# Reordering the last three tiles of an FP4 FFN: one down product moved behind the last gate and up products, the last tile quantised and transposed in two column ranges

## The reference

```python
def fp4_quant_dequant(x):          # blocks of 16 along the last dim
    scale = jnp.maximum(jnp.max(jnp.abs(xb), axis=-1, keepdims=True) / 6.0, 1e-12)
    idx = jnp.searchsorted(_MID, jnp.abs(xb / scale))
    return (_GRID[idx] * jnp.sign(xn) * scale).reshape(shape)
def fp4_linear(x, w):
    return jnp.einsum('bsk,nk->bsn', fp4_quant_dequant(x), fp4_quant_dequant(w))
h = jax.nn.silu(fp4_linear(x, w_gate)) * fp4_linear(x, w_up)     # 512 -> 1408
out = x1 + gb * fp4_linear(h, w_down)                            # 1408 -> 512
```

## Time and profile before

| | us |
|---|---|
| three runs | 2029.9, 2030.3, 2032.15 |
| median | 2030.3 |
| the profiled execution | 2029.9 |
| its span in the trace | 2027.6 |
| TensorE busy in the span | 1947.3 (96%) |
| VectorE busy | 1705.7 (84%) |
| GpSimd busy | 1211.9 (60%) |
| ScalarE busy | 626.6 (31%) |
| mean granted TensorE clock (1 = 2.4 GHz) | 0.983 |

### The profile page before, as it was taken

How to read it: one execution, slowest core, us unless ns; L and a number is a source line. 1 busy time by engine, 2 the same in 40 slices (tenths; PEclk the granted TensorE clock), 3 DMA queues, 4 the chain that set the end, 5 groups by cost and what they waited for, 6 DMA issues and landing times.

```text
span 2027.6 us, 27098 instructions
## 1 busy us (share of the span) xinstructions
PE 1947.3 (96%) x9401; PEld 930.6 (46%) x9401; DVE 1705.7 (84%) x2080; ACT 626.6 (31%) x878; POOL 1211.9 (60%) x1083
## 2 busy tenths in 40 slices
PE   4889999999999999999999999999999999999996
PEld 2334444444444444444444444444444444444442
DVE  4767676868767999999999999999999999999974
ACT  2234343433322323233233233332332333323321
POOL 2245454646444667677677676676776766767721
PEclk7999999999999999999999999999999999999998
DMA  7945646464643343333433433434334334333242
GB/s 252 292 112 160 183 130 172 141 174 130 180 111 99 68 103 70 83 91 70 91 84 70 104 70 81 95 71 89 87 70 102 73 77 98 70 86 88 65 85 49
DMA packets 417867, 219.26 MB, mean 108 GB/s; under 512 B 356214, under 2 KB 356226, under 8 KB 417804
## 3 DMA queue, kind: packets, MB, share of 16 engines
q1 hardware_dynamic: 417804, 218.44, 43.1%
HBM read 96.48 MB, written 33.57 MB: 64 GB/s over the span
## 4 chain that ended last, share of the span: by engine, by line
PE 81%; DVE 6%; SPq 4%; DMA 3%; issue 3%; POOL 2%; ACT 1%; POOLq 0%; DVEq 0%; ACTq 0%
PE bank L892 44%; PE bank L913 22%; PE bank L839 14%; SPq L355 2%; SPq L419 2%; DMA arena<-arena 1%; PE bank L864 1%; DVE arena L963 1%; DVE arena L1072 1%; DMA arena<-in_L_attn_W_qkva_dram 1%; DMA arena<-in_L_ffn_w_down_dram 1%; DMA arena<-in_L_ffn_w_up_dram 1%; POOL arena L508 1%; POOL arena L506 0%; DVE arena L1099 0%
## 5 line engine op out<-in xcount | busy, mean ns | idle before, releaser
L892 PE MATMUL bank<-wgu_hi,arena 128*128 128x512 f16 (+1 forms) x3072 | 870.0, 362 | 0.0
L892 PE MATMUL bank<-wgu_lo,arena 128*128 128x512 f16 (+1 forms) x1536 | 555.5, 362 | 0.0
L839 PE MATMUL bank<-arena,wq_hi 128*128 128x512 f16 x1536 | 463.5, 384 | 15.2 <-DMA arena<-arena 8.4
L913 PE MATMUL bank<-wd_hi,arena 128*128 128x512 f16 x1408 | 432.4, 381 | 18.1 <-DMA arena<-arena 18.1
L892 PEld LDWEIGHTS bank<-wgu_hi,arena 128*128 128x128 f16 x3072 | 300.8, 98 | 308.1 <-issue 0.5
L839 PE MATMUL bank<-arena,wq_lo 128*128 128x512 f16 x768 | 294.2, 383 | 0.0
L913 PE MATMUL bank<-wd_lo,arena 128*128 128x512 f16 x704 | 268.5, 381 | 0.0
L839 PEld LDWEIGHTS bank<-arena,wq_hi 128*128 128x128 f16 x1536 | 151.0, 99 | 196.5 <-issue 17.5
L603 POOL TENSOR_TENSOR arena<-arena 128x512 f32<-128x512 f32 x64 | 154.1, 2408 | 123.9 <-DVE arena L1241 123.9
L913 PEld LDWEIGHTS bank<-wd_hi,arena 128*128 128x128 f16 x1408 | 138.5, 98 | 187.3 <-DMA arena<-arena 14.0
L892 PEld LDWEIGHTS bank<-wgu_lo,arena 128*128 128x128 f16 x1536 | 150.4, 98 | 153.9 <-issue 0.2
(11 more groups left out here) (129 smaller groups left out, 2602.9 us busy)
## 6 DMA issues: line engine op xcount, KB each, us to landing
arena<-in_L_attn_x_dram SPq DMA_DIRECT2D x32, 1024.0 KB, 6.4
arena<-x_scratch SPq DMA_DIRECT2D x128, 256.0 KB, 3.2
x_scratch<-arena SPq DMA_DIRECT2D x16, 1024.0 KB, 4.4
out_dram<-arena SPq DMA_DIRECT2D x64, 256.0 KB, 3.0
arena<-in_L_wmod_dram SPq DMA_DIRECT2D x6, 1024.0 KB, 8.8
arena<-in_L_attn_W_qkva_dram SPq DMA_DIRECT2D x1, 3072.0 KB, 15.1
wgu_hi<-in_L_ffn_w_gate_dram SPq DMA_DIRECT2D x1, 2816.0 KB, 13.5
wgu_lo<-in_L_ffn_w_up_dram SPq DMA_DIRECT2D x1, 2816.0 KB, 10.4
```

The lines of the kernel that those rows point to most:

```text
L839: last = pe.matmul(dst[m % 2][:, :].rearrange("p (j t) -> p j t", j=NJ), w[:, k, at], uT[p][:, half, :, k, :], start=(n == 0), stop=(n == ...
L892: last = pe.matmul(dst[n][:, 0:w], xT[p][:, half, k, :], wt[:, k, cut], start=(m == 0), stop=(m == 3 * KD - 1))
L913: last = pe.matmul(d_bank[p][:, :], hT[p][:, half, k, :], wt[:, k, :], start=(m == 0), stop=(m == 3 * KF - 1))
```

## The change

Only the last three tiles (61, 62 and 63, `LAST = 63`) are touched. The loops over all other tiles issue what they issued.

- TensorE: tile 63 no longer has `down(61)` between its first and second chunk. After the tile come `down(61)`, `down(62)` and `down_last()`. `down_last` has the 33 matmuls of `down(63)`, with the 22 on the high half first and the 11 on the low half behind them; each part waits for its own two transposes.
- VectorE: in tile 62 `gate_out(61)` is left out. Tile 63 is `last_tile()`: the quantisation runs over the column ranges `H_PARTS` = 0 to 1024 and 1024 to 1408. The first range goes as far as `h_y` before the third chunk's `hidden`; `gate_out(61)` comes between `h_quantised` and `h_lo`. After the tile follow `gate_out(62)`, `gate_out(63)` and the residual addition of tile 63.
- ScalarE: in tile 63 `steps_of_h` and `h_hi` are issued for each range; the third chunk's `silu` stands behind the first range's `steps_of_h`.
- GpSimd: `ffn_add_x(61)` moves behind tile 63, and `ffn_add_x(63)` is gone (VectorE does it).
- SP: `turn_h(63)` becomes four transposes (8 and 3 blocks of the high half, 8 and 3 of the low half), each with its own wait. `store(61)`, `load_residual(63)` and `store(62)` are issued behind them.

```diff
+                def turn_last():
+                    wait(sp, down_ready, LAST - 1)
+                    sp.nop(nofuse=True)
+                    for half, done, loaded in ((0, h_hi_ready, last_hi_loaded), (1, h_lo_ready, last_lo_loaded)):
+                        for n, (c0, c1) in enumerate(H_PARTS):
+                            sp.wait_ge(done, LAST + 1 + n)
+                            sp.nop(nofuse=True)
+                            sp.dma_start(hT[1][:, half, c0 // P:c1 // P, :], h_half[1][:, half, c0:c1],
+                                         transpose=True).then_inc(loaded, 16)
...
-                for t in range(NTA - 7, NTA):
+                for t in range(NTA - 7, LAST - 1):
                     slot(t, t % 2)
-                store(NTA - 1, 1)
+                turn_h(LAST - 1, 0)
+                turn_last()
+                store(LAST - 2, 1)
+                load_residual(LAST, 1)
+                store(LAST - 1, 0)
+                sp.wait_ge(last_x2_ready, 1)
+                sp.dma_start(out_tile[LAST], gated[1]).then_inc(out_stored[1], 16)
...
                 def tile(i, p, b, first, last, b3, b4):
+                    if b == B - 1 and last:
+                        for n, (c0, c1) in enumerate(H_PARTS):
+                            silu(i, p, b, n + 1)
+                            steps_of_h(i, p, n, slice(c0, c1))
+                        for n, (c0, c1) in enumerate(H_PARTS):
+                            h_hi(i, p, n, slice(c0, c1))
+                        return
...
+                def down_last():
+                    pe.wait_ge(last_hi_loaded, 16 * len(H_PARTS))
+                    pe.wait_ge(gated_ready, LAST - 1)
+                    for k in range(KF):
+                        for wt in (wd_hi, wd_lo):
+                            pe.matmul(d_bank[1][:, :], hT[1][:, 0, k, :], wt[:, k, :],
+                                      start=(k == 0 and wt is wd_hi), stop=False)
+                    pe.wait_ge(last_lo_loaded, 16 * len(H_PARTS))
+                    for k in range(KF):
+                        last = pe.matmul(d_bank[1][:, :], hT[1][:, 1, k, :], wd_hi[:, k, :],
+                                         start=False, stop=(k == KF - 1))
...
-                    if not (isinstance(i, int) and i < 2):
+                    if not (isinstance(i, int) and (i < 2 or i == LAST)):
                         down(i - 2, p)
...
-                down(NTA - 2, 0)
-                down(NTA - 1, 1)
+                down(LAST - 2, 1)
+                down(LAST - 1, 0)
+                down_last()
...
+                def last_tile():
+                    at = [(n, slice(c0, c1)) for n, (c0, c1) in enumerate(H_PARTS)]
+                    for n, cut in at:
+                        hidden(LAST, 1, B - 1, n + 1)
+                        h_max(LAST, 1, n, cut)
+                        h_scale(LAST, 1, n, cut)
+                        h_recip(LAST, 1, n, cut)
+                        if cut.stop == F:
+                            h_largest(LAST, 1, n)
+                            h_power(LAST, 1)
+                        h_y(LAST, 1, n, cut)
+                    for n, cut in at:
+                        h_magic(LAST, 1, n, cut)
+                        h_round(LAST, 1, n, cut)
+                    for n, cut in at:
+                        h_quantised(LAST, 1, n, cut)
+                    gate_out(LAST - 2, 1, B - 1)
+                    for n, cut in at:
+                        h_lo(LAST, 1, n, cut)
...
                 tiles(dve, tile)
-                gate_out(NTA - 1, 1, B - 1)
+                gate_out(LAST - 1, 0, B - 1)
+                gate_out(LAST, 1, B - 1)
+                dve.wait_ge(x_res_loaded[1], 8 * (LAST - 1) + 16)
+                dve.wait_ge(gated_ready, LAST + 1)
+                dve.tensor_tensor(gated[1], gated[1], x_res[1], ALU.add).then_inc(last_x2_ready, 1)
```

More of the change, by code:

```diff
@@ L303, in adaln_block_kernel @@
         NTA = B * NT
+        LAST = NTA - 1
+        H_PARTS = ((0, 2 * GT), (2 * GT, F))
         g_bank, up_bank, d_bank = [bank[n] for n in (0, 4, 1)], [bank[n] for n in (2, 5, 3)], bank[6:8]
@@ L623, in tile @@
                         ffn_adaln(i + 4, p, b4)
-                    if not (isinstance(i, int) and i < 1):
+                    if not (isinstance(i, int) and (i < 1 or i >= LAST - 1)):
                         ffn_add_x(i - 1, 1 - p)
                 tiles(pool, tile)
-                ffn_add_x(NTA - 1, 1)
+                ffn_add_x(LAST - 2, 1)
+                ffn_add_x(LAST - 1, 0)
             @block.scalar
@@ L916, in down @@
                     last.then_inc(down_ready, 1)
+                def down_last():
[9 more added lines that the diff above has]
+                                         start=False, stop=(k == KF - 1))
+                    last.then_inc(down_ready, 1)
                 pe.wait_ge(wT_loaded, 16 * W_TURNS * (NGA - 1))
@@ L1222, in h_round, with h_y @@
[L1222 to L1227, removed]
+                def h_y(i, p, n=0, cut=WHOLE):
+                    nb = h_blocks(cut)
+                    dve.wait_ge(hq_recip_ready, i + 1 + n)
+                    dve.scalar_tensor_tensor(blocks(h[p][:, cut]), blocks(h[p][:, cut]), UNDER_ONE,
+                                             r_h[:, nb].unsqueeze(2).broadcast_to([P, nb.stop - nb.start, BLOCK]),
+                                             ALU.mult, ALU.mult).then_inc(hq_y_ready, 1)
@@ L1228, in h_quantised @@
+                def h_quantised(i, p, n=0, cut=WHOLE):
+                    nb = h_blocks(cut)
+                    dve.wait_ge(hq_grid_ready, i + 1 + n)
                     dve.wait_ge(hq_minus_scale_ready, i + 1)
-                    dve.tensor_tensor(blocks(h[p]), blocks(h[p]), sn_h[p].unsqueeze(2).broadcast_to([P, NBF, BLOCK]),
+                    dve.tensor_tensor(blocks(h[p][:, cut]), blocks(h[p][:, cut]),
+                                      sn_h[p][:, nb].unsqueeze(2).broadcast_to([P, nb.stop - nb.start, BLOCK]),
@@ L1230, in h_quantised, with h_lo @@
                                       ALU.mult).then_inc(hq_ready, 1)
-                def h_lo(i, p):
-                    dve.wait_ge(h_hi_ready, i + 1)
-                    dve.tensor_tensor(h_half[p][:, 1, :], h[p], h_half[p][:, 0, :], ALU.subtract).then_inc(h_lo_ready, 1)
+                def h_lo(i, p, n=0, cut=WHOLE):
+                    dve.wait_ge(h_hi_ready, i + 1 + n)
+                    dve.tensor_tensor(h_half[p][:, 1, cut], h[p][:, cut], h_half[p][:, 0, cut],
+                                      ALU.subtract).then_inc(h_lo_ready, 1)
@@ L1308, in tile @@
                 def tile(i, p, b, first, last, b3, b4):
+                    if b == B - 1 and last:
+                        last_tile()
+                        return
                     if isinstance(i, int) and i == 0:
@@ L1341, in tile @@
                     x_step(x_lo)
-                    if not (b == 0 and first):
+                    if not (b == 0 and first or isinstance(i, int) and i == LAST - 1):
                         gate_out(i - 1, 1 - p, b - first)
```

56 lines of the change are left out of this document (32 added, 24 removed).

## The result

The changed kernel's median is 2019.57 us (2016.88 to 2020.73, four runs), the kernel before's in the same comparison 2030.1. The two medians differ by 10.5 us. The ratio of the runs is 0.9939, 95% interval 0.9918 to 0.9961: 12.4 us faster, between 7.9 and 16.6. The forecast was 9.9 us.

The account below looks back on a forecast made before the run. TensorE, busy 96%, was bound at the end by a 13.25 us wait for tile 63's transpose. Gains of 8.5, 0.8 and 0.6 us, 9.9 together, took 2029.9 to 2020.0; plus 0.4 for the median, 2020.4 us, range 2018.4 to 2023.2.

Parts of the forecast that it names:

- What bounds the end, and which way it goes: At the kernel's end TensorE waits 13.25 us for tile 63's quantisation and transpose; the change makes it faster, chance 0.94.
- The restart 8.5 us earlier: TensorE begins down(63) when the 3-block high transpose lands, at 2004.2 instead of 2012.74.
- h_lo(62) at 1.61 us: On VectorE, h_lo of tile 62 takes 1.61 us instead of 2.32, GpSimd's addition having moved away.
- One fixed cost for four transposes, not four: Tile 63's four transposes overlap their fixed cost of some 2 us; counted once, the high half lands at 2004.2.
- The serial rival: Each small transpose starts only when the one ahead has landed: high range two 1.8 us later, 2022.2 us; chance 0.12.
- the slower one: Transposes cost the same whatever their size and run one after another: 2033.5 us, or 2039.5 at the longest; chance 0.02.
- The low halves landed in time: Low-half transposes land by 2007.4, hidden behind the 22 high matmuls, which last until 2008.9 even at full clock.
- The clock term 0.8: Down(63) loses 2.0 us (1.4 to 2.8) to the low clock after a 4.7 us idle time, gaining 0.8.
- The end 0.6: Tile 63's last addition takes 0.68 us on VectorE instead of 1.26 on GpSimd, gaining 0.6 (0 to 0.7).
- The sum 9.9: Earlier transposes 8.5, less time at the low clock 0.8 and the addition 0.6 together gain 9.9 us.
- Everything in front of tile 61 is unchanged: Nothing ahead of tile 61 gains or loses time; the forecast counted only the kernel's end.
- the 1.6 us of VectorE's wait for the third silu: In tile 63 VectorE idles 1.6 us between h_y of 1024 columns and hidden of 384, awaiting ScalarE's silu.

Follow-up runs that it names:

- e7: Changed kernel with tile 63's residual addition back on GpSimd; from tile 62's maxima to the span's end 46.07 us, against 45.29 in the changed kernel.
- e9: Changed kernel with the third chunk's silu ahead of the first range's steps on ScalarE; from tile 62's maxima to the span's end 41.90 us against 45.29.
- e3: Changed kernel without column ranges: last tile quantised at full width, two transposes of 11 blocks, high half first; ratio 0.9936 to the kernel before.
- e2: Changed kernel reduced to the new product order: full-width quantisation, one transpose of 22 blocks, last addition on GpSimd; ratio 0.9963 to the kernel before.
- e4: Changed kernel with hidden, maxima, scales and reciprocals at full width, ranges from h_y on, silus first; median 2015.47 us, ratio 0.9915 to the kernel before.
- e11: Changed kernel plus 10 filler matmuls on TensorE between down(62) and down(63); from tile 62's maxima to the span's end 45.32 us against 45.29.
- e8: e4 plus a semaphore letting down(63) begin when the first high range has landed; median 2014.97 us, ratio 0.992 to the kernel before.

## Why the prediction was right or wrong

- **What bounds the end, and which way it goes: right.** The chain, the place of the wait and the sign were as told.
- **The restart 8.5 us earlier: 8.87** (41.04 to 32.17). Hidden of the third chunk started at 1991.75 on the ruler of the kernel before (1992.06 less the shift of 0.31), where I had 1991.7. The error lies behind it: from there to the first issue I had 8.9 us, measured 8.3. What was off is the 0.04 us that I put between any two instructions. It fits where a pass waits for the one ahead: h_magic of 1024 columns at 1994.55 and h_round of the same at 1995.80 are 1.25 us apart for a pass of 1.22. Two passes over different ranges don't wait for each other, and the next starts ahead of the recorded end of the last: h_round of 1024 columns at 1995.80 and h_magic of 384 at 1996.96 are 1.16 us apart for a pass of 1.24. Three such pairs (each 0.12 us shorter than I had it) give 0.36 us of the 0.6; the rest is small differences and rounding up. The transpose of 3 blocks landed in 2.4 us where I had 2.3.
- **h_lo(62) at 1.61 us: right, 1.63.** GpSimd's addition was gone from beside it, and the 2.32 of the earlier trace rows with it: 2.32 in both profiles of the kernel before, 1.62 or 1.63 in all eleven of the other kernels. The Trainium skill (SBUF — State Buffer, Who interferes with whom) says that such a VectorE operation and a GpSimd operation contend; these durations agree with it. By the longer one the chain would have been 0.7 late. Nor was h_lo(63) held up: it ended at 2002.05, and the GpSimd instruction that started beside it (L617, one column) took 1.12 us where its counterpart L597 took 0.19 in the kernel before.
- **One fixed cost for four transposes, not four: right.** The four were issued in 5.20 us without a pause and the second landed 3.7 us after the first one's issue. The serial rival (5.4 us after it) falls, and with it the slower one. The low halves landed in time, as told: no gap lies ahead of the 23rd matmul.
- **The clock term 0.8: 0.95.** The loss is 1.69 us (9.02 against 7.33 with the clock kept), I had 2.0 out of 1.4 to 2.8. The 7.16 us for down(63) without a loss was 0.17 too short.
- **The end 0.6: 0.79.** Measured by e7 as 0.78, of which the addition's duration is 0.57, as told. I had kept 2.8 us from the store's issue to the end of the span, and it is 2.5; why stays open.
- **The sum 9.9: 10.6 in the profiles, 10.5 and 9.8 between the medians, 12.4 and 11.2 by the ratios.** All three terms were a little small, 0.7 us together. With the measured terms the sum would have given 2019.7, well inside the range, so they are not what put 2017.9 outside it.
- **The step that failed: "Everything in front of tile 61 is unchanged", a term put at nothing, and the range built on it.** No instruction there was changed, and no lasting shift shows (the first silu starts at 643.91 and 639.91 before, 644.03 and 640.25 after). But its time is not one number. The start of tile 62's maxima moves by 3.9 us between two profiles of the kernel before, by 3.8 between two of the changed kernel, and lies between 1967.83 and 1978.36 in all thirteen. I took one execution as its time, and 0.4 us as all that separates that from a median. Single runs of the kernel before lie 9 us apart (2026.57 to 2035.25), and the intervals of the ratios are 4 to 9 us wide. A range of 4.8 us that held only the uncertainties of the end left nothing for this. Whether a measurement with such a scatter falls into the range is partly luck: the ratio, 1.8 us more than the tail shows, fell 0.5 us below it, and the median fell inside. Where the 1.8 us lie, if they are more than scatter, stays open. The three runs that I was shown, 2.3 us from lowest to highest, were too few to see this from; the clock losses at 100 and 142 us in the earlier trace rows were the hint that I read only as a price.
- **What I had right and undervalued:** the 1.6 us of VectorE's wait for the third silu stood in the sum, but I didn't ask what the column ranges bring in return. The third chunk's product is there at 1985.3, ahead of VectorE, so nothing is gained by beginning with the first two chunks. What the ranges do bring comes later in the chain, 1.1 us (e9 against e3), and in the change that is less than the wait costs.

## What to carry to other kernels

When the last unit of a pipeline hangs on a long chain of another engine, move whole products behind it that need nothing from it: here (e2) that started tile 63's maxima 5.7 us earlier with no matmul more. Split a chain by what its consumer needs first (here the high half) and not by what its producer delivers first, unless the producer really is late. Ranges pay where the next engine can begin on the first of them: from h_y on they brought the restart 2.0 us forward (e4 against e3). And put the in-order neighbour engine's calls in the order in which they become ready. Measure an edit of a few microseconds from an event that the edit leaves alone: the tail repeats to 0.2 us where whole runs scatter by 9.

## What I had not expected of the hardware

The length of TensorE's idle time doesn't decide alone whether its clock falls. It was kept after 2.79 us (e9) and lost after 2.30 (e11):

```profile
2003.24 0.39 PE L954 MATMUL bank<-wd_hi,arena 128*128 128x512 f16 x1 [2.79 <-DMA arena<-arena]
```

```profile
2001.18 0.39 PE L953 MATMUL bank<-wd_hi,arena 128*128 128x512 f16 x1 [2.30 <-DMA arena<-arena]
```

After the 2.79 the windows of e9 read 1.00 all through down(63); in e11 the clock fell while TensorE was already at work again, and cost the same 1.7 us as after 4.4:

```profile
2001.00:2002.00 1.00, 0.82 (x3) 0.82 0.82 162
2002.00:2003.00 1.00, 1.00 (x4) 0.50 1.01 194
```

At the end of the kernel the clock was kept after idle times of 1.3 us (twice), 1.8 and 1.9, but in the attention part of the kernel before it fell at 294.4 after one of only 1.75 us, ended by VectorE at 293.39:

```profile
293.39 1.39 PE L864 MATMUL bank<-ident,arena 128*128 128x128 f32 x8 [1.75 <-DVE arena L1087]
```

So between 1.75 and 2.79 us of idle time these traces show both outcomes, and no run here says what decides. The gain of e4, e8 and e9 through the clock is seen in one profile each; for e4 and e8 the differences of the medians fit it, but don't show it.
